# Two VectorE steps exchanged in an attention loop, and eight DMA transposes per unit added to the sync queue

## The reference, cut to what matters

```python
x = x + einsum('bsi,boi->bso', x, weight[adapter_ids])        # one of 16 matrices per sequence
# attention: 32 query heads, 8 key/value heads, head size 128
q, k, v = x @ Wq.T, x @ Wk.T, x @ Wv.T
q, k = rope(rmsnorm(q) * q_norm_w), rope(rmsnorm(k) * k_norm_w)
k_all = concat([k_cache[block_table], k]); v_all = concat([v_cache[block_table], v])   # 512 + 128 keys
scores = q @ k_all.T / sqrt(128); cached keys past the sequence's length are masked
x = x + softmax(scores) @ v_all @ Wo.T
```

## Time and profile before

| | |
|---|---|
| time, median of 3 runs | 1181.11 us (1179.0 to 1181.77) |
| profiled execution | 1181.4 us, of which its span is 1179.6 us |
| TensorE (PE) busy | 1130.6 us, 96% of the span |
| weight loads (PEld) | 977.7 us, 83% |
| GpSimd (POOL) busy | 874.3 us, 74% |
| VectorE (DVE) busy | 789.3 us, 67% |
| ScalarE (ACT) busy | 664.2 us, 56% |
| granted TensorE clock, mean | 0.994 |
| DMA | 71.22 MB in 176128 packets |

### The profile page before, as it was taken

How to read it: one execution, slowest core, us unless ns; L and a number is a source line. 1 busy time by engine, 2 the same in 40 slices (tenths; PEclk the granted TensorE clock), 3 DMA queues, 4 the chain that set the end, 5 groups by cost and what they waited for, 6 DMA issues and landing times.

```text
span 1179.6 us, 22933 instructions
## 1 busy us (share of the span) xinstructions
PE 1130.6 (96%) x6540; PEld 977.7 (83%) x6540; DVE 789.3 (67%) x1793; ACT 664.2 (56%) x1886; POOL 874.3 (74%) x925
## 2 busy tenths in 40 slices
PE   6899999999999999999999999999999999999997
PEld 5578878888888888888888888888888888888886
DVE  6476576666767667676776667676676666766664
ACT  3354556655656556565656556565565655665553
POOL 2776767877877777787787777787787777778771
PEclk9899999999999999999999999999999999999999
DMA  6634322113121122212221121211312112211110
GB/s 191 177 84 130 99 69 71 27 33 79 36 68 34 33 73 46 64 28 63 54 66 31 35 76 38 70 30 32 76 43 64 31 35 73 76 35 36 48 37 27
DMA packets 176128, 71.22 MB, mean 60 GB/s; under 512 B 154241, under 2 KB 154370, under 8 KB 176002
## 3 DMA queue, kind: packets, MB, share of 16 engines
q1 hardware_dynamic: 166464, 51.20, 18.6%
q0 software_dynamic: 8192, 16.79, 5.2%
q10 hardware_dynamic: 1346, 1.76, 0.4%
HBM read 67.56 MB, written 2.10 MB: 59 GB/s over the span
## 4 chain that ended last, share of the span: by engine, by line
PE 79%; issue 9%; DVE 7%; ACT 2%; SPq 1%; DMA 0%; POOL 0%; ACTq 0%; DVEq 0%
PE S L815 18%; PE T L756 11%; PE O L750 5%; PE O L752 5%; PE O L751 5%; PE Q L750 5%; PE Q L751 5%; PE Q L752 5%; PE Y L750 4%; PE Y L752 4%; PE Y L751 4%; DVE pr L594 3%; PE KV L752 3%; PE KV L750 2%; PE KV L751 2%
## 5 line engine op out<-in xcount | busy, mean ns | idle before, releaser
L430 ACT ACTIVATE pr<-pr,nb 128x640 f32<-128x640 f32 x256 | 213.5, 834 | 174.9 <-DVE nb L594 147.1
L300 POOL DMA_INDIRECT rawv<-in_vrows,kidx x256 | 262.8, 1026 | 63.5 <-issue 62.5
L318 POOL TENSOR_SCALAR pr<-pr,rc 128x640 f32<-128x640 f32 x256 | 207.4, 818 | 126.4 <-DVE rc L601 126.2
L524 DVE TENSOR_TENSOR ptl<-T,pth 128x512 fp32r<-128x512 f32 x320 | 214.1, 686 | 129.1 <-issue 82.8
L397 ACT ACTIVATE pth<-T 128x512 fp32r<-128x512 f32 x320 | 177.4, 596 | 156.7 <-PE T L756 147.7
L594 DVE CUSTOM_DVE_ANT_0 pr<-S,mask,rst 128x640 f32<-128x640 f32 x256 | 224.6, 877 | 11.0 <-PE S L815 6.1
L756 PE MATMUL T<-ident,pr 128*128 128x128 f32 x1280 | 171.1, 272 | 0.0
L756 PEld LDWEIGHTS T<-ident,pr 128*128 128x128 f32 x1280 | 151.4, 140 | 9.6
L815 PE MATMUL S<-kh,qh 128*128 128x320 f32 x512 | 130.7, 336 | 23.4 <-DVE nb L594 14.2
L815 PEld LDWEIGHTS S<-kh,qh 128*128 128x128 f32 x512 | 87.2, 190 | 63.8 <-DVE nb L594 31.4
L750 PE MATMUL O<-pth,vh 128*128 128x512 f32 x256 | 112.1, 438 | 6.7 <-DVE ptl L524 6.7
(11 more groups left out here) (102 smaller groups left out, 2471.7 us busy)
## 6 DMA issues: line engine op xcount, KB each, us to landing
wraw<-in_wall SPq DMA_DIRECT2D x75, 256.0 KB
rawk<-in_kt SPq DMA_DIRECT2D x1024, 16.0 KB
lws<-in_lw SPq DMA_DIRECT2D x28, 256.0 KB, 4.1
rawv<-in_vrows,kidx POOLq DMA_INDIRECT x256
acc<-in_x SPq DMA_DIRECT2D x8, 256.0 KB, 4.4
out<-acc SPq DMA_DIRECT2D x8, 256.0 KB
xts<-in_xt SPq DMA_DIRECT2D x7, 256.0 KB, 2.8
wraw<-in_wall ACTq DMA_DIRECT2D x5, 256.0 KB
```

The costliest lines, as they stand in the source:

```text
L300: e.indirect_dma_start(out=rawv[:, v % 2, t, :], out_offset=None, in_=vrows, in_offset=bass.IndirectOffsetOnAxis(ap=kidx[:, hk % 2, NT * b ...
L318: e.tensor_scalar(pr[:, u % 2, g, :], pr[:, u % 2, g, :], rc[:, u % 2, g:g + 1], 1.0, ALU.mult, ALU.mult).then_inc(g_norm, 1)
L430: e.activation(pr[:, u % 2, g, :], pr[:, u % 2, g, :], ACT.Exp, bias=nb[:, u % 2, g:g + 1], scale=-1.0, accum_out=sm[:, u % 2, g:g + 1]).t ...
L524: return e.tensor_tensor(dst, src, hi.bitcast(F32), ALU.subtract)
```

## The change

SP's loop issues, in each of the iterations 8 to 63, eight DMA transposes of `mask[:, b, :]` (128 partitions by 640 two-byte numbers, 160 KB) into one of three slots of a new tile `spare`, after the K loads and ahead of the weight loads. Nothing reads `spare`. The transpose number n waits until number n - 3 has landed. At the end SP waits for all 448. On VectorE `largest(i, 2)` now stands ahead of `p_lo(w, 2)`. The on-chip memory set aside for the descriptors of GpSimd's DMAs is halved from 8192 to 4096 bytes of a partition.

```diff
+        spare = sb("spare", [P, 3, 5, P], BF16)
...
+        d_turn = slots("d_turn", 3)
...
                 if i + 2 < NU:
                     for t in range(NT):
                         load_kt(i + 2, t)
+                if NB <= i < NU:
+                    for n in range(8 * (i - NB), 8 * (i - NB) + 8):
+                        if n >= 3:
+                            e.wait_ge(d_turn[n % 3], 16 * (n // 3))
+                        e.dma_start_transpose(spare[:, n % 3, :, :], mask[:, b, :]
+                                              ).then_inc(d_turn[n % 3], 16)
                 if i + 3 < NB:
                     load_x(i + 3)
...
             e.wait_ge(d_out, 16 * NB)
+            for n in range(3):
+                e.wait_ge(d_turn[n], 16 * len(range(n, 8 * (NU - NB), 3)))
...
                 if i == -1:
                     masks((0,))
-                if turn:
-                    p_lo(w, 2)
                 if i > 0 and real:
                     largest(i, 2)
+                if turn:
+                    p_lo(w, 2)
...
-                   dynamic_dma_scratch_size=8192)
+                   dynamic_dma_scratch_size=4096)
```

More of the change, by code:

```diff
@@ L703, in _ @@
                     masks((0,))
+                if i > 0 and real:
+                    largest(i, 2)
                 if turn:
                     p_lo(w, 2)
-                if i > 0 and real:
-                    largest(i, 2)
                 if nxt:
```

## The result

The changed kernel takes 1425.63 us (median of 4 runs, 1422.27 to 1427.04) against 1180.64 us of the kernel before on the same chip: a ratio of 1.2072, 95% interval 1.2046 to 1.2099. It is slower, as forecast, but by 245 us and not 45, and the time lies above the stated range.

A forecast was written before the change was run, and what follows sets the result against it. TensorE, with one hole per period, bounds the kernel before; with the transposes SP does. Time = (1181.4 - 37.6) + 53 x 1.77 - 12 = 1226 us, 1.77 being SP's excess per unit over the new 16.63 us period; range 1142 to 1400.

The forecast's parts named there:

- one hole per period: TensorE idles ahead of the fourth head's scores, then runs its matmuls slower: 0.66 us in each of 57 periods.
- SP's part without transposes: SP's work per unit on page numbers, K loads and weight loads: 10.9 us, leaving 5.7 us of room.
- The exchange: On VectorE, `largest(i, 2)` ahead of `p_lo(w, 2)` fits into idle time and removes TensorE's hole: gain 37.6 us.
- SP becomes the bound: SP's transposes exceed its room, so waits for `kl` vanish and ScalarE or GpSimd waits for K loads; chance 0.38.
- c: Time SP is held issuing one transpose: taken as 0.46 us, with ends 0.33 and 1.71.
- X: Time SP stays in one unit's eight transposes, waits for landings included: 7.5 us.
- L: Time from a transpose's issue to its landing: taken as 3.1 us, from plain 256 KB loads.
- D: Time one transpose takes of the DMA engines: 0.84 us, eight 6.7 us; the engines hold.
- the lead: How far SP's loads start ahead of their use, hiding the first lateness: 12 us.
- Rival 2: On SP the transpose issue itself is long, because many small blocks are written out: 1327 to 1554 us; chance 0.19.
- Rival 1: On-chip data lands sooner, SP is never late and only the exchange counts: 1144 us, at worst 1166; chance 0.36.
- Rival 3: The transposes' traffic delays other transfers, such as GpSimd's last gather: about 1200 us; chance 0.03.

The follow-up runs named there:

- x_plain8: The changed kernel with its eight transposes per unit replaced by eight plain copies of the same 160 KB, same waits; 1164.92 us, ratio 0.9852.
- x_mix: The changed kernel with transposes of 128, 256, 384, 512 and 640 columns in turn instead of always 640; 1413.55 us (one run).
- x_t8_onek: The changed kernel, eight transposes per unit kept, with K of a unit loaded by one DMA without page lookup; 1136.19 us, ratio 0.9619.
- x_onek: The kernel before with VectorE's two steps exchanged, no transposes, and K of a unit loaded by one DMA without page lookup; 1136.23 us, ratio 0.9614.
- t_only: The changed kernel with VectorE's two steps put back in the old order, so the transposes alone; 1426.77 us, ratio 1.2086.

## Why the prediction was wrong

- **The bound of the kernel before**: right. TensorE with one hole per period, SP as an engine with its own budget. SP's part without transposes, 10.9 us, was too low: with SP as the bound it is 11.7, since the loads of page numbers ahead of K take 1.0 us and not 0.6, and the K loads 10.0 in the mean and not 9.7.
- **The exchange**: right in mechanism, place and what comes next; 43 us instead of 37.6, 3.6 of the difference being waits for `ptl` that I expected to stay. The new period was forecast as 16.63 and is 16.65.
- **SP becomes the bound**: right, with the signs named: the waits for `kl` gone, ScalarE waiting for K loads.
- **"Issue, c: ... I take 0.46, the median of a DMA of that size"**: this is the step that failed. It measured 1.28 us, and 1.32 from one start to the next. A transpose is not issued like a copy of its size. In x_plain8 the copy of the same bytes took 0.48, so the row was right for a copy and the wrong row for this operation. (The 0.46 is the distance of starts of 256 KB loads in the earlier trace rows; their median in the earlier trace rows is 0.43.)
- **X = 2L + D + c = 7.5 us**: wrong in form as well. The formula supposes that SP waits for landings, with L = 3.1. The landings that the trace records come 2.7 us after the start of a transpose in the median; with 1.32 us an issue three of them take 4.0, the landing was over by then, and X is simply eight issues, 8 x 1.32 = 10.6, with the long ones 10.8 in the mean. With the measured c alone the formula would still have given 6.2 + 0.84 + 1.28 = 8.3 and 1269 us: it lacks the case in which the issues follow one another without a wait. For plain copies its form was right: x_plain8 lands after 2.1 us, the formula gives 5.5, and the set shown took 5.3.
- **The sum**: with everything measured it is 1138 + 53 (10.76 + 11.67 - 16.65) - 18 = 1426 us, where 11.67 is U less X. Of the miss of 200 us, X has 53 (10.76 - 7.5) = 173 and SP's part without transposes 53 (11.67 - 10.9) = 41. The exchange takes off 6, the lead, which is 16 to 19 us and not 12, another 6. So c, with the form that it gives to X, is the step that took the time out of the range; the 41 us alone would have left it inside.
- **Rival 2**, the long issue, was what happened, with 0.19 and a price of 1327 to 1554. Its reason was wrong: what grows with the number of blocks is 0.01 us per 128 columns, the rest is fixed (x_mix). The upper end of the range came from half of this rival; the longest issue of the earlier trace rows, 1.71 us, was the honest end for c, and the range should have taken it in, since no row of a transpose spoke for the near end.
- **Rival 1**, it fits: decided the other way by the same c. **Rival 3**, traffic: false here, even with a DMA share of 0.66. **The engines' price D** was sized well: from the queue's share on the two pages (0.438 x 1424.4 - 0.186 x 1179.6) / 448 = 0.90 us, against 0.84. It and the halved descriptor memory cost nothing (x_t8_onek against x_onek).

Three slips in the numbers change nothing in the forecast. The rows on SP's waits in the earlier trace rows are those of a window from 170 us on, not 165. Rival 1 with a gain of 22.5 us is 1159 us, not 1166. And the 1337 us for an issue of 1.07 us do not come from the forecast's own sum, which gives X = 8.1 and 1258; rival 2's form of X gives 1334.

What stays open: why an issue is that long. The runs show that it does not come from the amount of data (x_mix). Nor do transposes that are queued already make it long: in the changed kernel the first of a set, behind the K loads, takes 1.22 us in the median, nearly as much as the later ones with 1.28. Behind the one large K load of x_t8_onek the first takes 2.0, so what is queued can add to it. What the sequencer does in 1.2 us no view shows. The single long issues have a companion in the trace: of the 15 of the changed kernel over 1.65 us, 14 overlap a packet of the DMA queue q8, which the page calls "instruction", against 19 of the other 433. No run took these packets away, so this is a coincidence in time and not a shown cause.

## What to carry to other kernels

Treat the queue that issues DMAs as an engine: add up the issue times of its loop, take the period of the bound engine, and the difference is the room; up to it a DMA is free, and beyond it every unit pays in full after a lead of a period or so. When a kind of DMA has no row in the trace, take its issue cost as unknown up to the longest issue seen, and let the range say so; size and landing of a similar copy say nothing of it. Count in what the queue does between its DMAs too: here it made the room 5.0 us and not 5.7. The best kernel here that computes the whole task is the exchange alone, 1137.94 us: a step that frees a tile for the bound engine goes ahead of one whose input is not there yet.

## What the runs showed of the hardware

- A DMA transpose issued from SP holds the sequencer 1.23 us at 128 columns, 1.28 at 640 and 1.38 at 1280 (medians of the lines or single rows), where a copy of 160 KB takes 0.48. The Trainium skill, "Advanced Engine Details and Errata", X-Bar Transpose, has transposes as fast as regular DMAs. The runs disagree in all three measures: the issue is 2.6 times as long, the landing comes 2.7 us after the start against 2.1, and the packets of one transpose take 0.90 us of each DMA engine against 0.47 for the copy (x_plain8: (0.367 x 1165.9 - 0.193 x 1136.2) / 448).
- 448 transposes, 73 MB, beside 71 MB of other traffic cost the compute engines nothing: DMA share 0.66, TensorE busy 952.19 us of 955 with and without them.
- TensorE's granted clock fell behind stops of TensorE (0.57 in 283 to 287 us, after 4.73 us of standing still), to a mean of 0.913 in the changed kernel from 0.994, and its busy time rose from 1130.6 to 1198.7 us. With SP as the bound it set no time: t_only ran at 0.925 and took 1.1 us more.
